# Scan output returned by scatters through the inverse rank, and earlier loads of the next input

## The chip, the cores and the metric

The kernel runs on one core of one Trainium2 chip. The core has TensorE (PE; its weight loads are shown apart as PEld), VectorE (DVE), ScalarE (ACT), GpSimd (POOL) and SyncE (SP), and 16 DMA engines that all of them share. The engines run their own instruction streams and wait for each other through semaphores. The metric is the device time of one execution in microseconds (us), as the median of three runs.

## The reference

The input is x, 8 images of 512 channels on a 32 x 32 grid (1024 tokens), float32. Four layers follow each other, each added to its input: `x = x + layer(gn(x))`, where `gn` normalises over 32 groups of channels.

- L0: a 5 x 5 map of correlations of each token with its neighbours is put beside the 512 channels, and a 1 x 1 convolution with ReLU follows.
- L1, the layer of this change: a projection to 3 x 512 channels (an input of the scan, a residual and a gate, each through SiLU); a convolution over three tokens; then, for each of two heads of 256 channels, the tokens are put in an order that the head's Moebius parameters give (`perm`), a selective scan with 8 states runs over them, and the result is put back in token order:

```
x_h = _gather_last(x_h, perm[None, :, None, :])
...
y_h = _selective_scan(x_h, dt, A, B_t, C_t, Dparam)
inv = jnp.argsort(perm, axis=-1)
y_h = _gather_last(y_h, inv[None, :, None, :])
y = y * jax.nn.silu(gate) + res
```

  Then an output projection with SiLU.
- L2 and L3: 1 x 1 convolutions with a bias.

The order depends on the parameters alone, so it is the same for all 8 images.

## The kernel before

Images are worked one after the other: image 0, then a loop of three passes over two images each (images 1 to 6), then image 7. Channels lie in `KC` = 4 chunks of 128 partitions, tokens in `NT` = 8 tiles of 128; `P` = 128, `DH` = 256 channels a head, `HEADS` = 2. x of the current image is in `X[z]`; the other buffer `X[1 - z]` is scratch for the scan's factors (`pfac`, `qfac`, `pT`, `qT`, one chunk each) until the next image's x is loaded into it. Large products are made in three passes of half-width parts (`passes`, L1522); the scan's products are in float32. Everything that TensorE does runs through one helper line, L1500, but for transposes. TensorE fills its waits in the scan with pieces of the input projection (`piece`, `filler`).

**Into scan order.** Once a token's row is complete (256 channels and 17 scan parameters, `ROW` numbers), GpSimd scatters the rows of each head to DRAM, eight indirect DMAs of 128 rows a head (L450); the destination of a row is `rank[token]`. SP loads each head back in scan order with one DMA (L353, 1092 KB) into `rows4[:, h]`.

**The scan.** `scan_sums`, `factor_rows`, `scan_inner` and `scan_y` on TensorE, with `scan_states` on DVE (the last of it is L1457, which adds `diag`, made by GpSimd in `diagonal(h)`, L456). `scan_y(h)` gives four pairs of tiles; ACT evicts each pair to `yscan`, a view of `buf_b` (L696, semaphore `y_ev`).

**Back to token order.** SP stores each pair of tiles to `d_y[h]`, in scan order (L357, semaphore `y_out`), four stores a head. When all four have landed, GpSimd gathers the rows by `rank`, eight indirect DMAs a head (L467), into `ytok[h]`, a view of the same SBUF as `rows4[:, h]`. Semaphores `y_in{h}{half}` count them by halves of four tiles. TensorE's `y_chunk(k, half)` (L1788) waits for `y_in{k // 2}{half}` and transposes four tiles back to channels: k = 0, 1 are head 0, k = 2, 3 are head 1. DVE multiplies the result with the gate (L1246) and adds the residual (L1248); the output projection reads that. `y_chunk(0, 0)` comes right behind `scan_y(1)`; `y_chunk(2, 0)` comes behind some of the input and output projection, and `y_chunk(2, 1)` later still.

**x of the next image.** SP loads its four chunks (512 KB each) behind the last `scan_y` product (`y_mm` 8), L363. In images 1 to 6 the next image's statistics come from an earlier load of their own (`early`), so only the normalisation on ACT (L556, L559) reads these chunks. Image 0 has no early load, and DVE takes the next image's statistics from them (`input_stats`, L882).

GpSimd's queue, in the order of its code: scatters of both heads, `diagonal(0)`, `diagonal(1)`, `gather(0)`, `gather(1)`, then memsets and small powers. SP's: rows of both heads, eight stores, four loads of x, the correlation's traffic of the next image, and stores of the output. In image 0 GpSimd waits for `p_rank` before each head's scatters, since the rank is still being counted on DVE.

Of the kernel before, what the change touches and what calls it, by code (L numbers as in the profile page):

```python
# [32 lines left out]
def constants():  # L33

    v = np.arange(P)
    parts = {}
    parts["ident"] = np.eye(P)
    parts["upto"] = v[:, None] <= v[None, :]
    parts["after"] = v[:, None] > v[None, :]
    same8 = (v[:, None] // T8) == (v[None, :] // T8)  # L40
    parts["same8"] = same8
    parts["after8"] = same8 & (v[:, None] > v[None, :])
    parts["group_mean"] = ((v[:, None] // 16) == (v[None, :] // 16)) / 16.0
    parts["ones"] = np.ones((P, P))
    blocks = [(s, size) for size in (128, 64, 32, 16) for s in range(0, P, size)]
    left, right = np.zeros((P, HEADS, G)), np.zeros((P, HEADS, G))
    keep = np.ones((P, HEADS))
    for h in range(HEADS):
        groups = [g for g in range(G) if g != FAR_GROUP[h]]
        for g, (s, size) in zip(groups, blocks):  # L50
            left[s:s + size // 2, h, g] = 1
            right[s + size // 2:s + size, h, g] = 1
        left[:, h, FAR_GROUP[h]] = right[:, h, FAR_GROUP[h]] = 1
        keep[FAR_GROUP[h] * S:(FAR_GROUP[h] + 1) * S, h] = 0
    parts["left"], parts["right"] = left, right
    parts["off_left"], parts["off_right"] = BIG * (1 - left), BIG * (1 - right)
    parts["keep"] = keep
    parts["within8"] = (v[:, None] % T8) <= np.arange(T8)[None, :]
    parts["eq8"] = (v[:, None] % T8) == np.arange(T8)[None, :]
    parts["block16"] = (v[:, None] // T8) == np.arange(P // T8)[None, :]  # L60
    n = np.arange(N).reshape(NT, P).T
    y, x = n // W, n % W
    inside = np.zeros((P, NT, 5, 5))
    for r in range(5):
        for c in range(5):
            inside[:, :, r, c] = ((y + r - 2 >= 0) & (y + r - 2 < H) & (x + c - 2 >= 0) & (x + c - 2 < W))
    parts["inside"] = inside

    step = np.arange(W - 1, dtype=np.float32) / np.float32(W - 1)
    line = np.concatenate([np.float32(-1) * (np.float32(1) - step) + step, [np.float32(1)]]).astype(np.float32)  # L70
    parts["grid"] = np.concatenate([line[x], line[y]], axis=1)
    at, cols = {}, []
    pos = 0
    for name, a in parts.items():
        a = np.asarray(a, np.float32).reshape(P, -1)
        at[name] = (pos, a.shape[1])
        pos += a.shape[1]
        cols.append(a)
    return at, np.concatenate(cols, axis=1)


def build(nc, d):
    at, packed = constants()
    with ExitStack() as ctx:
# [43 lines left out]
        rank = sb("rank", [P, HEADS, NT], I32)  # L128
        deq8 = sb("deq8", [P, HEADS, T8])
# [30 lines left out]
        def scratch(z):  # L160
# [31 lines left out]
        d_scan = [nc.dram_tensor(f"d_scan{h}", (N, ROW), F32, kind="Internal").ap() for h in range(HEADS)]  # L192
        d_score = [nc.dram_tensor(f"d_score{h}", (P, NT), F32, kind="Internal").ap() for h in range(HEADS)]
# [13 lines left out]
            yt_mm y_gate y_res silu2 half_in""".split()  # L207
# [12 lines left out]
                   y_out0=64, y_out1=64, y_in00=8 * NT, y_in01=8 * NT, y_in10=8 * NT, y_in11=8 * NT, yt_mm=2 * KC, y_gate=2 * KC, y_res=2 * KC, silu2=8)  # L220
# [67 lines left out]
        def _(eng):  # L288
# [49 lines left out]
            def image(m, z, last=False):  # L338
# [15 lines left out]
                for h in range(HEADS):  # L354
                    for j in range(4):
                        wait(eng, "y_ev", m, 4 * h + j + 1)
                        eng.dma_start(d_y[h].rearrange("(c p) r -> p c r", p=P)[:, 2 * j:2 * j + 2, :],  # L357
                                      yscan[:, h, 2 * j:2 * j + 2, :]).then_inc(s[f"y_out{h}"], 16)
                if not last:

                    wait(eng, "y_mm", m, 4 * HEADS)
                    for k in range(KC):
                        eng.dma_start(X[1 - z][:, k, :], d["x"][bass.ds(m + 1, 1), k * P:(k + 1) * P, :].rearrange("a p n -> (a p) n")).then_inc(s["x_in"], 16)  # L363
# [21 lines left out]
        def _(eng):  # L385
# [40 lines left out]

            def image(m, z, last=False):
# [15 lines left out]
                for h in range(HEADS):  # L443
# [5 lines left out]
                    for t in range(NT):  # L449
                        eng.indirect_dma_start(d_scan[h], bass.IndirectOffsetOnAxis(ap=rank[:, h, t:t + 1], axis=0),  # L450
                                               rows4[:, h, t, :], None).then_inc(s[f"scattered{h}"], 16)
                def diagonal(h):
# [8 lines left out]
                def gather(h):  # L461

                    wait(eng, f"y_out{h}", m, 64)
                    wait(eng, "y_mm", m, 4 * (h + 1))
                    eng.nop(nofuse=True)
                    for t in range(NT):
                        eng.indirect_dma_start(ytok[h][:, t, :], None, d_y[h],  # L467
                                               bass.IndirectOffsetOnAxis(ap=rank[:, h, t:t + 1], axis=0)).then_inc(s[f"y_in{h}{2 * t // NT}"], 16)

                diagonal(0)  # L470
                diagonal(1)
                gather(0)
                gather(1)
# [39 lines left out]
        def _(eng):  # L513
# [33 lines left out]
            def normalize(m, g, k, x, by_chunk=False):  # L547
# [5 lines left out]
                if k == 0 and g == 2:  # L553
                    wait(eng, "y_out0", m, 64)
                    wait(eng, "y_out1", m, 64)
# [942 lines left out]
        def _(eng):  # L1498
# [114 lines left out]
            def image(m, z, last=False):  # L1613
# [163 lines left out]
                def y_chunk(k, half):  # L1777
# [5 lines left out]
                    wait(eng, f"y_in{k // 2}{half}", m, 8 * NT)  # L1783
# [175 lines left out]
```

## Time and profile before

| | |
|---|---|
| median of 3 runs | 1817.06 us (1812.06 to 1821.29) |
| the profiled execution | 1825.13 us |
| its span in the profile | 1823.3 us |
| TensorE busy | 1719.2 us, 94% |
| VectorE, ScalarE, GpSimd busy | 1088.6, 866.5, 416.0 us |
| memory | 140.15 MB moved, mean 77 GB/s |

Times in the profile count from the span's start. Image 0's scan lies at about 150 to 230 us, and the later ones follow at intervals of some 217 us: image 2 has its scan output at 619 to 660 us, image 3 at 835 to 877 us. A row of a timeline gives start, duration, engine, line, operation, what it writes and reads, and in brackets the idle time of the engine before it with what ended it. Ends of matmuls are modelled, so a busy TensorE is not one at its peak, and its own idle time is what can be won.

### The profile page before, as it was taken

Reading aid. Unit: us, or ns where it says so; the run is one execution under the profiler, and the core shown is the slowest. Engines: PE = TensorE matmul, PEld = TensorE weight load, DVE = VectorE, ACT = ScalarE, POOL = GpSimd, SP = SyncE. Lnnn points to the kernel's source line nnn. Section 1 sums busy time; section 2 is a strip of 40 time slices with the busy share of each in tenths; the row PEclk is TensorE's granted clock in tenths of the full one; section 3 lists DMA queues with packets and bytes.
Section 4 is the critical chain, followed back from the end, with each engine's and each line's share of the span. In section 5 each row is a group of like instructions: output and inputs, shape, how many; then the busy total and the mean of one; then the engine's idle time right before and its main releaser. Section 6 shows DMA issues by size and latency. Waiting matters only on the chain.

```text
span 1823.3 us, 23722 instructions
## 1 busy us (share of the span) xinstructions
PE 1719.2 (94%) x8573; PEld 949.8 (52%) x8573; DVE 1088.6 (60%) x2136; ACT 866.5 (48%) x1057; POOL 416.0 (23%) x425
## 2 busy tenths in 40 slices
PE   4498999999999999999999999999999999999998
PEld 3154554555545554556545565455554555555643
DVE  6778575555754666546665547555575466652665
ACT  4665245554255534454534643555425653445432
POOL 0403301133022321132120430113302232113220
PEclk9799999999999999999999999999999999999999
DMA  6203410233112231133201341023311132112201
GB/s 210 80 1 99 139 39 16 87 113 116 38 68 68 97 103 34 71 110 108 69 14 70 122 139 39 13 89 115 116 38 65 65 101 102 39 46 93 76 24 46
DMA packets 124055, 140.15 MB, mean 77 GB/s; under 512 B 52243, under 2 KB 101459, under 8 KB 123934
## 3 DMA queue, kind: packets, MB, share of 16 engines
q1 hardware_dynamic: 109886, 103.18, 17.8%
q0 software_dynamic: 12288, 34.68, 5.7%
q8 instruction: 72, 1.18, 0.3%
q10 hardware_dynamic: 1760, 0.71, 0.2%
q14 instruction: 49, 0.40, 0.1%
HBM read 78.52 MB, written 60.01 MB: 76 GB/s over the span
## 4 chain that ended last, share of the span: by engine, by line
PE 67%; DVE 10%; issue 9%; DMA 5%; ACT 4%; POOL 2%; another core or an unknown queue 2%; SPq 0%; DVEq 0%; POOLq 0%; ACTq 0%
PE bank L1500 64%; DMA rows<-d_scan 2%; DMA rows<-d_norm 1%; DVE bn L882 1%; POOL d_scan L450 1%; PE bank L1721 1%; DVE gate L1246 1%; PE bank L1788 1%; DVE gate L1060 1%; PE bank L1666 1%; DMA d_scan<-rows,rank 1%; DVE res L1180 1%; DVE res L1178 1%; DVE x_even L1152 1%
## 5 line engine op out<-in xcount | busy, mean ns | idle before, releaser
L1500 PE MATMUL bank<-buf_a,win_hi 128*128 128x512 f16 x1536 | 461.6, 382 | 8.1 <-DVE buf_a L954 8.1
L1500 PE MATMUL bank<-buf_a,win_lo 128*128 128x512 f16 x768 | 293.2, 382 | 0.0
L1500 PE MATMUL bank<-buf_b,w_hi 128*128 128x512 f16 x960 | 287.5, 381 | 2.8 <-DVE buf_b L954 2.8
L1500 PEld LDWEIGHTS bank<-buf_a,win_hi 128*128 128x128 f16 x1536 | 150.2, 99 | 190.0 <-issue 22.0
L1500 PE MATMUL bank<-gate,w_out 128*128 128x512 f32 x512 | 229.2, 594 | 5.1 <-DVE gate L1248 5.1
L450 POOL DMA_INDIRECT d_scan<-rows,rank x128 | 125.9, 984 | 357.4 <-DVE rows L1215 314.6
L1500 PE MATMUL bank<-buf_b,w_lo 128*128 128x512 f16 x480 | 183.3, 382 | 0.0
L1500 PE MATMUL bank<-buf_a,w_hi 128*128 128x512 f16 x576 | 171.3, 379 | 1.4 <-DVE x_odd L1152 1.4
L1500 PEld LDWEIGHTS bank<-gate,w_out 128*128 128x128 f32 x512 | 94.4, 190 | 112.3 <-issue 98.8
L1500 PEld LDWEIGHTS bank<-buf_b,w_hi 128*128 128x128 f16 x960 | 93.9, 99 | 112.4 <-DVE buf_b L954 3.5
L467 POOL DMA_INDIRECT rows<-d_y,rank x128 | 121.8, 952 | 133.1 <-DMA d_y<-buf_b 97.6
L1500 PEld LDWEIGHTS bank<-buf_a,win_lo 128*128 128x128 f16 x768 | 75.7, 99 | 92.4 <-issue 3.0
L1246 DVE TENSOR_TENSOR gate<-bank,gate 128x512 f32<-128x512 f32 x64 | 43.9, 685 | 130.0 <-PE bank L1788 90.2
L605 ACT ACTIVATE res<-bank,par 128x512 f32<-128x512 f32 x64 | 48.6, 775 | 139.4 <-issue 77.0
L394 POOL TENSOR_TENSOR st<-st,minus_half 128x4 f32<-128x4 f32 x30 | 30.9, 1029 | 343.1 <-DVE st L940 257.0
L1500 PE MATMUL bank<-buf_a,w_lo 128*128 128x512 f16 x288 | 109.1, 379 | 0.0
L954 DVE TENSOR_TENSOR buf_a<-work,buf_a 128x1024 f16<-128x1024 f32 x68 | 83.0, 1221 | 28.9 <-ACT work L559 28.6
L954 DVE TENSOR_TENSOR buf_b<-work,buf_b 128x1024 f16<-128x1024 f32 x60 | 73.3, 1222 | 41.9 <-ACT work L559 33.4
L605 ACT ACTIVATE buf_b<-bank,par 128x512 f32<-128x512 f32 x64 | 49.7, 776 | 91.1 <-PE bank L1500 91.1
L1500 PEld LDWEIGHTS bank<-buf_a,w_hi 128*128 128x128 f16 x576 | 56.0, 99 | 64.3 <-DVE x_odd L1152 1.8
L594 ACT ACTIVATE work<-bank,par 128x512 f32<-128x512 f32 x64 | 43.2, 683 | 93.1 <-PE bank L1500 93.1
L578 ACT ACTIVATE corr<-bank 96x512 f16<-96x512 f32 x16 | 9.5, 591 | 158.1 <-PE bank L1568 158.1
(227 smaller groups left out, 2921.2 us busy)
## 6 DMA issues: line engine op xcount, KB each, us to landing
rows<-d_scan SPq DMA_DIRECT2D x16, 1092.0 KB, 5.9
d_y<-buf_b SPq DMA_DIRECT2D x64, 256.0 KB, 2.1
work<-in_x SPq DMA_DIRECT2D x24, 512.0 KB, 4.6
d_gram<-rows SPq DMA_DIRECT2D x32, 260.0 KB, 2.4
x_even<-in_x SPq DMA_DIRECT2D x16, 512.0 KB
x_odd<-in_x SPq DMA_DIRECT2D x16, 512.0 KB
out_x<-x_even SPq DMA_DIRECT2D x16, 512.0 KB, 2.7
out_x<-x_odd SPq DMA_DIRECT2D x16, 512.0 KB, 2.6
```

Source lines behind the costliest of these rows:

```text
L394: eng.tensor_tensor(st[g][:, :, 4], st[g][:, :, 3], minus_half.broadcast_to([P, KC]), ALU.pow).then_inc(s[f"gn_rstd{g}"], 1)
L450: eng.indirect_dma_start(d_scan[h], bass.IndirectOffsetOnAxis(ap=rank[:, h, t:t + 1], axis=0), rows4[:, h, t, :], None).then_inc(s[f"scatt ...
L467: eng.indirect_dma_start(ytok[h][:, t, :], None, d_y[h], bass.IndirectOffsetOnAxis(ap=rank[:, h, t:t + 1], axis=0)).then_inc(s[f"y_in{h}{2 ...
L594: act(tmp[:, u % 3, :], ps[out_bank[u]][:, :], ACT.Silu, bias=par[:, BOUT + o:BOUT + o + 1]).then_inc(s["out_evac"], 1)
L605: act(dst, ps[in_bank[q]][:, :], ACT.Silu, bias=par[:, col:col + 1], scale=inv("in")).then_inc(s["in_evac"], 1)
L882: eng.bn_stats(bn[g][:, k, half, :], x[:, k, half * HALF:(half + 1) * HALF]).then_inc(s[f"gn_raw{g}"], 1)
L954: TT(lo[:, k, :], normed[:, k % 2, :], hi[:, k, :], ALU.subtract).then_inc(s[f"gn_split{g}"], 1)
L1060: TS(cmp_row[:, :, start:start + n], others, own[:, t:t + 1], 0.0, op, ALU.add, counts[:, a, q:q + 1]).then_inc(s["p_count"], 1)
L1152: STT(X[z][:, o, c], ps[(l2_bank if stage == 2 else l3_bank)[u]][:, :], par[:, INV + stage:INV + stage + 1], X[z][:, o, c], ALU.mult, ALU. ...
L1178: STT(dst, src[:, 0:N], w[0], dst, ALU.mult, ALU.add).then_inc(s["conv_mac"], 1)
L1246: TT(gate[:, k, c], ps[yt_bank[k][half]][:, :], gate[:, k, c], ALU.mult).then_inc(s["y_gate"], 1)
L1500: return eng.matmul(out, lhsT, rhs, start=start, stop=stop, skip_group_check=True, **kw)
```

## The change

GpSimd no longer gathers. `y_scatter(h, j)` waits for one eviction and scatters its two tiles of 128 rows from `yscan` to `d_y[h]`, at the token's own place. The index is `order`, the inverse of `rank`, in scan order: entry p of tile c is the token at that place of the scan. SP then loads a head of `d_y` in token order with two plain DMAs of 512 KB, one for each `y_in` semaphore (`y_load(h)`), when all eight scatters of the head have landed. The eight stores on SP go. On GpSimd the first two pairs of head 0 are placed in front of `diagonal(1)`.

SP loads chunks 0 to 2 of the next x after `y_load(0)` and `dh_mm` 8 (the last product that reads `pfac`; `qfac` and `pT` are done by then too), chunk 3 after `y_mm` 8, and `y_load(1)` after that.

In image 0 alone `order` is made: GpSimd scatters the token numbers (a new constant, `token`, rows of 8 bytes) by `rank` to `d_order`, 16 indirect DMAs in three places, and SP loads both heads from there.

```diff
+    parts["token"] = np.repeat(n[:, :, None], 2, axis=2).astype(np.int32).view(np.float32)
...
+        order = sb("order", [P, HEADS, NT, 2], I32)
...
-                for h in range(HEADS):
-                    for j in range(4):
-                        wait(eng, "y_ev", m, 4 * h + j + 1)
-                        eng.dma_start(d_y[h].rearrange("(c p) r -> p c r", p=P)[:, 2 * j:2 * j + 2, :],
-                                      yscan[:, h, 2 * j:2 * j + 2, :]).then_inc(s[f"y_out{h}"], 16)
+                if first:
+                    eng.wait_ge(s["order_out"], 16 * NT * HEADS)
+                    for h in range(HEADS):
+                        eng.dma_start(order[:, h], d_order[h].rearrange("(c p) r -> p c r", p=P)).then_inc(s["order_in"], 16)
+
+                def y_load(h):
+
+                    wait(eng, f"y_out{h}", m, 16 * NT)
+                    for half in range(2):
+                        t = slice(half * NT // 2, (half + 1) * NT // 2)
+                        eng.dma_start(ytok[h][:, t, :], d_y[h].rearrange("(t p) r -> p t r", p=P)[:, t, :]).then_inc(s[f"y_in{h}{half}"], 16)
+
+                def x_load(k):
+
+                    eng.dma_start(X[1 - z][:, k, :], d["x"][bass.ds(m + 1, 1), k * P:(k + 1) * P, :].rearrange("a p n -> (a p) n")).then_inc(s["x_in"], 16)
+
+                y_load(0)
                 if not last:
-
+                    wait(eng, "dh_mm", m, 4 * HEADS)
+                    for k in range(KC - 1):
+                        x_load(k)
                     wait(eng, "y_mm", m, 4 * HEADS)
-                    for k in range(KC):
-                        eng.dma_start(X[1 - z][:, k, :], d["x"][bass.ds(m + 1, 1), k * P:(k + 1) * P, :].rearrange("a p n -> (a p) n")).then_inc(s["x_in"], 16)
+                    x_load(KC - 1)
+                y_load(1)
+                if not last:
                     correlation(m + 1)
...
+            def order_out(h, tiles):
+
+                for t in tiles:
+                    eng.indirect_dma_start(d_order[h], bass.IndirectOffsetOnAxis(ap=rank[:, h, t:t + 1], axis=0),
+                                           const("token")[:, 2 * t:2 * t + 2].bitcast(I32), None).then_inc(s["order_out"], 16)
...
+                    if first:
+                        order_out(0, range(5 * h, 5 + 3 * h))
...
-                def gather(h):
-
-                    wait(eng, f"y_out{h}", m, 64)
-                    wait(eng, "y_mm", m, 4 * (h + 1))
+                def y_scatter(h, j):
+
+                    wait(eng, "y_ev", m, 4 * h + j + 1)
                     eng.nop(nofuse=True)
-                    for t in range(NT):
-                        eng.indirect_dma_start(ytok[h][:, t, :], None, d_y[h],
-                                               bass.IndirectOffsetOnAxis(ap=rank[:, h, t:t + 1], axis=0)).then_inc(s[f"y_in{h}{2 * t // NT}"], 16)
+                    for c in (2 * j, 2 * j + 1):
+                        eng.indirect_dma_start(d_y[h], bass.IndirectOffsetOnAxis(ap=order[:, h, c, 0:1], axis=0),
+                                               yscan[:, h, c, :], None).then_inc(s[f"y_out{h}"], 16)
 
                 diagonal(0)
+                if first:
+                    order_out(1, range(NT))
+                    eng.wait_ge(s["order_in"], 16 * HEADS)
+                y_scatter(0, 0)
+                y_scatter(0, 1)
                 diagonal(1)
-                gather(0)
-                gather(1)
+                y_scatter(0, 2)
+                y_scatter(0, 3)
+                for j in range(4):
+                    y_scatter(1, j)
```

The counts of the semaphores follow: `y_out` is now 16 a scatter, and ACT's wait for it before the third normalisation and TensorE's wait for `y_in` are adapted to that.

## Rows read from the trace of the kernel before

**Rows 1.** The page's part 1: busy us (share of the span) and instructions.
```profile
PE 1719.2 (94%) x8573; PEld 949.8 (52%) x8573; DVE 1088.6 (60%) x2136; ACT 866.5 (48%) x1057; POOL 416.0 (23%) x425
```

**Rows 2.** Stretches: us, busy of each engine, granted clock, DMA share, GB/s.
```profile
220.00:230.00 10.00, 8.34 (x27) 4.03 (x26) 8.05 (x21) 1.45 (x3) 2.05 (x7) 1.00 0.09 25
625.00:842.00 217.00, 212.42 (x1071) 117.78 (x1070) 126.87 (x242) 104.53 (x128) 50.16 (x52) 1.00 0.25 78
```

**Rows 3.** Waits of TensorE, 625 to 680 us: total us, times, longest.
```profile
PE bank L1500 <- DVE gate L1248: 0.5, 1, 0.5
PE bank L1500 <- issue: 0.5, 1, 0.5
```

**Rows 4.** Waits of all engines over the whole span.
```profile
POOL rows L467 <- DMA d_y<-buf_b: 97.6, 16, 10.4
...
PEld bank L1788 <- issue: 12.7, 48, 0.3
```

**Rows 5.** Timeline of ScalarE: evictions of the scan output in images 2 and 3.
```profile
619.08 0.60 ACT L696 ACTIVATE buf_b<-bank 128x512 f32<-128x512 f32 x1
...
639.41 0.60 ACT L696 ACTIVATE buf_b<-bank 128x512 f32<-128x512 f32 x1 [1.92 <-PE bank L1500]
...
854.88 0.60 ACT L696 ACTIVATE buf_b<-bank 128x512 f32<-128x512 f32 x1 [0.52 <-issue]
```

**Rows 6.** Timeline of weight loads: the transposes of L1788 in images 2 and 3.
```profile
643.47 1.92 PEld L1788 LDWEIGHTS bank<-cst,rows 128*128 128x128 f32 x16
...
655.30 0.14 PEld L1788 LDWEIGHTS bank<-cst,rows 128*128 128x128 f32 x1 [0.24 <-issue]
...
660.47 0.14 PEld L1788 LDWEIGHTS bank<-cst,rows 128*128 128x128 f32 x1 [0.24 <-issue]
...
871.48 0.14 PEld L1788 LDWEIGHTS bank<-cst,rows 128*128 128x128 f32 x1 [0.24 <-issue]
```

**Rows 7.** Timeline of image 2: scatters into scan order, before and behind them.
```profile
575.80 0.36 DVE L1215 TENSOR_TENSOR rows<-rows 128x64 f32<-128x64 f32 x2
...
577.00 1.06 POOL L450 DMA_INDIRECT d_scan<-rows,rank  x1 [37.13 <-DVE rows L1215]
...
597.79 0.96 POOL L450 DMA_INDIRECT d_scan<-rows,rank  x1 [0.30 <-issue]
...
600.29 0.38 SPq L353 DMA_DIRECT2D rows<-d_scan  x1
```

**Rows 8.** Timeline of image 2: `diagonal(1)`, its reader, and two gathers of head 1.
```profile
623.68 1.97 POOL L456 TENSOR_TENSOR work<-md,cst 128x1024 f32<-128x1024 f32 x1 [13.52 <-DVE md L1432]
...
634.00 1.27 DVE L1457 TENSOR_TENSOR work<-bank,work 128x512 f32<-128x512 f32 x2
...
648.89 0.94 POOL L467 DMA_INDIRECT rows<-d_y,rank  x1 [0.30 <-issue]
...
651.38 0.95 POOL L467 DMA_INDIRECT rows<-d_y,rank  x1 [0.30 <-issue]
```

**Rows 9.** DMA issues at 570.8, 571.3, 600.3 and 702.9 us: KB, us to landing.
```profile
work<-in_x SPq DMA_DIRECT2D x1, 512.0 KB, 3.3
work<-in_x SPq DMA_DIRECT2D x1, 512.0 KB, 4.1
rows<-d_scan SPq DMA_DIRECT2D x1, 1092.0 KB, 5.8
rows<-d_norm SPq DMA_DIRECT2D x1, 532.0 KB, 3.8
```

**Rows 10.** Timeline of image 0: GpSimd, the first transpose, and DVE behind x.
```profile
152.29 0.96 POOL L450 DMA_INDIRECT d_scan<-rows,rank  x1 [7.13 <-DVE rank L1069]
...
166.91 1.96 POOL L456 TENSOR_TENSOR work<-md,cst 128x1024 f32<-128x1024 f32 x1 [3.62 <-DVE md L1432]
...
206.62 1.92 PEld L1788 LDWEIGHTS bank<-cst,rows 128*128 128x128 f32 x16
...
216.37 2.47 DVE L882 BATCH_NORM_STATS2 bn<-x_odd 128x6 f32<-128x512 f32 x4 [3.50 <-DMA x_odd<-in_x]
```

More of the change, by code:

```diff
@@ L192, in build @@
         d_scan = [nc.dram_tensor(f"d_scan{h}", (N, ROW), F32, kind="Internal").ap() for h in range(HEADS)]
+        d_order = [nc.dram_tensor(f"d_order{h}", (N, 2), I32, kind="Internal").ap() for h in range(HEADS)]
         d_score = [nc.dram_tensor(f"d_score{h}", (P, NT), F32, kind="Internal").ap() for h in range(HEADS)]
@@ L206, in build @@
             fac_mv fac_mm fac_arg fac_exp fac_gam fac_pq fac_8 fac_diag fac_tp fac_ptq mm_m m_ev dh_mm h_zero h_st y_mm y_ev y_out0 y_out1 y_in00 y_in01 y_in10 y_in11
-            yt_mm y_gate y_res silu2 half_in""".split()
+            yt_mm y_gate y_res silu2 half_in order_out order_in""".split()
         gn_names = [f"gn_{what}{g}" for g in range(4) for what in ("raw", "stat", "sum", "var", "rstd", "bias", "hi", "norm", "split")]
@@ L219, in build @@
                    m_ev=2 * HEADS, dh_mm=4 * HEADS, h_zero=1, h_st=7 * HEADS, y_mm=4 * HEADS, y_ev=4 * HEADS,
-                   y_out0=64, y_out1=64, y_in00=8 * NT, y_in01=8 * NT, y_in10=8 * NT, y_in11=8 * NT, yt_mm=2 * KC, y_gate=2 * KC, y_res=2 * KC, silu2=8)
+                   y_out0=16 * NT, y_out1=16 * NT, y_in00=16, y_in01=16, y_in10=16, y_in11=16, yt_mm=2 * KC, y_gate=2 * KC, y_res=2 * KC, silu2=8)
         for g in range(4):
@@ L553, in normalize @@
                 if k == 0 and g == 2:
-                    wait(eng, "y_out0", m, 64)
-                    wait(eng, "y_out1", m, 64)
+                    wait(eng, "y_out0", m, 16 * NT)
+                    wait(eng, "y_out1", m, 16 * NT)
                 act((a_hi if g == 3 and by_chunk else gn_hi_of[g])[:, k, :], x[:, k, :], ACT.Identity, bias=st[g][:, k, 5:6], scale=st[g][:, k, 4:5]).then_inc(s[f"gn_hi{g}"], 1)
@@ L1782, in y_chunk @@
                         wait(eng, "y_ev", m, 4 * HEADS)
-                    wait(eng, f"y_in{k // 2}{half}", m, 8 * NT)
+                    wait(eng, f"y_in{k // 2}{half}", m, 16)
                     if k >= 2:
```

## The prediction

> **What bounds the kernel now.** First the page's busy times [rows 1]: TensorE is busy for 1719.2 of 1823.3 us. Its clock is not the issue: in a steady image the granted clock is 1.00, the 2.4 GHz level [rows 2]. A window of 217 us over one whole image (the third, called image 2) has TensorE busy for 212.4 us [rows 2]. Some 4.6 us an image are idle, and this is the most that a steady image can win.
>
> Next the waits of TensorE in image 2 while the scan output travels [rows 3]: 0.5 us for a gate multiplication, 0.5 us for issue, none for the returning rows. Over the whole run the transposes of L1788 waited 12.7 us in 48 places, each time "issue" and at most 0.3 us [rows 4]. GpSimd waited 97.6 us for the d_y stores [rows 4], which looks like the cost to remove, but TensorE names GpSimd's rows nowhere. The return path is hidden today. The question is whether it stays hidden, because the change also alters its length.
>
> **Head 0.** The first eviction of head 0 ends at 619.68 [rows 5]; SP stores, GpSimd gathers, and TensorE reaches `y_chunk(0, 0)` at 643.47 [rows 6]. After the change each pair of scatters follows its eviction. The trace has scatters of the same kind: L450 moves 128 rows an instruction, 0.96 us and 0.30 us between two, so eight last 7 x 1.26 + 0.96 = 9.8 us; the first starts 0.84 us after the last work that it waits for (576.16 to 577.00); and SP reacts 1.54 us after the end of the last one (598.75 to 600.29) [rows 7]. The rows now have 1024 instead of 1092 bytes, so I take these durations as they are. Head 0: start 619.68 + 0.84 = 620.5, four scatters to 625.3, `diagonal(1)` (1.97 us [rows 8]) to 627.6, four more to 632.7, plus 1.54 = 634.2, when SP issues two loads. `diagonal(1)` moves from 623.68 to about 625.6; its reader L1457 starts at 634.00 [rows 8], so 8.4 us of cover shrink to 6.4. Cost 0; without that cover, 2 us.
>
> For the plain load of half a head (512 KB) I have: 532 KB in rows of 532 bytes, 3.8 us from issue to landing; 512 KB in 4 KB rows 3.3 us, and the next one, issued 0.5 us later, 4.1 us; a whole head (1092 KB) 5.8 us [rows 9]. I take 3.8 us for the first half, since its 1 KB rows are nearest to the first kind, and 5.6 for both. Head 0 is in by 640, 3 us before TensorE wants it. Cost 0.
>
> **Head 1, the tight one.** From the end of its first eviction to `y_chunk(2, 0)` there are 15.3 us in image 2 (640.01 to 655.30) and 16.0 in image 3 (855.48 to 871.48) [rows 5, 6]. The same two places read in the other images give 15.2 for images 0, 1, 5 and 7 and 16.4 for 4 and 6. Today the fourth gather is issued by 652.33 [rows 8] and its half is in before TensorE comes. After the change half 0 needs all eight scatters and then a load: 0.84 + 9.8 + 0.3 (three more waits, one in front of a pair, 0.1 us each as my guess below the 0.30 us pause) + 1.54 + 3.8 + 0.05 for the last semaphore = 16.3 us. TensorE stands 1.1 us in images 0, 1, 2, 5 and 7, 0.3 in image 3, and 0 in images 4 and 6: 5.8 us. TensorE works in order and is full behind this point, so a steady image doesn't take a stall back. Half 1 is wanted 5.2 us later (660.47 [rows 6]) and lands 1.8 us after half 0: no cost. What is late next are the gates of chunks 2 and 3 and the out projection behind them, by the same time.
>
> Bounds: with the load at 3.3 us and no pause between pairs, 15.5 us, a stall of 0.3 in five images, 1.5 us in all. With the load at 5.8 us, 18.3 us: 3.1 x 5 + 2.3 + 1.9 x 2 = 21.6 us.
>
> The page "DMA: Bandwidth & Descriptors" of the Trainium skill (Anatomy of one DMA) gives about 2.0 us plus the bytes at 436 GB/s, an estimate of 3.2 us for this load. This case's loads are slower than that rule [rows 9]; by the rule the stall would be 0.5 in five images, 2.5 us in all.
>
> **The x loads.** Three of four chunks leave after `dh_mm` 8 instead of `y_mm` 8, on SP right behind `y_load(0)`, so at about 635 instead of 644; the fourth stays; all are in before `y_load(1)` is issued near 652. In a steady image TensorE waits for nothing that comes from x there [rows 3]: gain 0. SP loses eight stores and gains four loads an image, with no work queued behind them that is near: cost 0. Without the early start the 2 MB would lie before `y_load(1)` all the same, so it isn't a cover that the sum needs.
>
> **Image 0.** Sixteen extra scatters of 8-byte rows. The first five fit into the 7.13 us in which GpSimd waits for the rank of head 1 (5 x 1.26 = 6.3) [rows 10]: cost 0. Three more, 3.8 us, lie in the 3.62 us before `diagonal(0)` [rows 10]: 0.2 us, covered. Eight more run from 169.4 to 179.2; then 1.54 us, then SP's two loads of 1024 tiny rows each. The trace has none; the nearest take 3.8 us (the 532-byte rows, as many) and 3.3 at the least [rows 9]. I take 3.8 plus 0.4 for the second, so `order` is in at 184.9. Head 0's scatters start near 185.8, end at 198.2 with the diagonal inside them; half 0 lands at 203.6 and half 1 at 205.4, against TensorE's 206.62 [rows 10]. Cost 0.2 as a middle, 0 to 2. The other way, DVE waited until 216.37 for x [rows 10], its statistics delayed the gates, and TensorE lost 1.7 us (8.34 of 10 busy from 220 to 230 [rows 2]). x now lands some 3 us sooner, which pays for this image's own 1.1 us. The constants' load grows by 8 KB once: nothing.
>
> **Sum.** 5.8 - 1.1 + 0.2 = +4.9, say +5 us on the profiled execution's 1825.13 us (span 1823.3), which lies 0.4% above the median of 1817.06. Taken over as a difference: 1822 us. A change of 0.5%, about 9 us, is what a measurement of this kernel can tell from none. So my forecast is "no change that can be told, on the slow side".
>
> **Rivals.**
> A, the forecast: stalls of about 1 us, total -1 to +12 us, 1816 to 1829. Chance 0.48, of which 0.13 falls beyond +9, since that needs only 16.8 us of path instead of 16.3.
> B, slower: both halves of a head land together, after 5.8 us. Then the 21.6 us above less 1.5 in image 0: +20, 1837 us. It decides once the first half takes over 4.3 us. For it: the whole-head load of 5.8 us. Against it: of two loads issued 0.5 us apart the first landed 1.3 us before the second [rows 9]. The same page of the Trainium skill (Queues, rings and completion order) says that each DMA engine consumes one queue's descriptors in ring order, which agrees. Chance 0.20.
> C: no stall, because half 0 comes in 3.3 us or less, and image 0 gains its 1.7 us: 1815 to 1818. Chance 0.18.
> D, faster: TensorE's idle time shrinks, since next image's normalisation no longer meets a late x and DVE's gates come sooner. It needs 1.1 of the 4.6 idle us in every image; no wait in [rows 3] names a load. 1806 us; chance 0.07.
> E, slower: DVE holds GpSimd off. Head 1's scatters run from 640.9 to 651, over the four gate additions of L1248, which read two SBUF tiles. Held 0.69 us by each, +2.8 us an image on top of A: 1844. Against it: the gather at 648.89 took 0.94 us over such an addition, and the one at 651.38, without one, 0.95 [rows 8]. The Trainium skill's "SBUF — State Buffer" describes an exclusive port lock between the two; this trace does not show it on indirect DMAs. Chance 0.07.
>
> **Numbers.** Same: 0.35 + 0.18 = 0.53. Slower: 0.13 + 0.20 + 0.07 = 0.40. Faster: 0.07. The likeliest case's own range is 1816 to 1829. The range for 8 in 10 takes in C below and most of B above: 1813 to 1839.
>
> **What the profile after would show.** Right: no wait before `y_chunk(0, 0)`; a wait of 0 to 1.5 us before `y_chunk(2, 0)` in most images, released by a DMA; scatters of 0.95 us with 0.3 to 0.4 us between; head 1's last one ending 10.7 to 11.1 us after its first eviction; half 0 landing 3.3 to 4.1 us after issue. Wrong: pairs that stand over 0.6 us apart, a half landing after 5 us (B), scatters over 1.2 us beside the gates (E), or idle TensorE time gone that now reads "gate" or "issue" (D). What would make me most wrong is a scatter whose write to HBM lands late because 2.5 MB of loads are queued beside it: all of head 0's loads and x are then in flight while head 1 is scattered.

## Result, and the profile after

| | before | after |
|---|---|---|
| median of 20 runs each | 1816.03 us (1812.06 to 1821.29) | 1820.44 us (1817.51 to 1824.05) |
| the profiled execution, its span | 1825.13, 1823.3 us | 1821.2, 1819.4 us |

The ratio is 1.0027, with a 95% interval from 1.0018 to 1.0035: 4.9 us slower (0.0027 x 1816). The forecast was +5 us, "no change that can be told, on the slow side". The sum came out, but the steps did not: its three terms were off by 2, 3 and 5 us, and the errors cancelled.

The shown execution of before was a long one for its kernel (1825.13 where the timed ones took 1812 to 1821). A kernel that has the change's constant, tensors and semaphores but uses none of them (`e4_alloc_only` below, 1816.5 us) is therefore the better picture of before, and its trace is used beside it. Lines moved: L474 scatters into scan order (L450 before), L448 makes `order`, L492 is `y_scatter`, L367 `y_load`, L371 `x_load`, L1820 the transposes of `y_chunk` (L1788), L1422 the scan's masks, on which TensorE waits when a scan begins.

The page of the kernel after, parts 1 and 6: GpSimd has sixteen instructions more than in [rows 1], and a load of half a head takes 4.4 us as a median over both halves.

```profile
PE 1717.9 (94%) x8573; PEld 951.3 (52%) x8573; DVE 1090.1 (60%) x2136; ACT 867.6 (48%) x1057; POOL 437.9 (24%) x441
...
rows<-d_y SPq DMA_DIRECT2D x32, 512.0 KB, 4.4
```

Waits of the kernel after over the whole span (us in total, times, longest):

```profile
POOL d_y L492 <- ACT buf_b L728: 125.0, 23, 10.6
...
PE bank L1532 <- DVE scan_tmp L1422: 16.3, 8, 3.7
...
PEld bank L1820 <- DMA rows<-d_y: 3.8, 8, 0.9
```

The second of these three waits, the one for the masks, in the trace of `e4_alloc_only`, that is, before:

```profile
PE bank L1503 <- DVE scan_tmp L1393: 9.3, 8, 2.1
```

GpSimd's 97.6 us of waiting for stores [rows 4] are gone and replaced by 125.0 us of waiting for evictions, and neither matters. The new wait for returning rows is 3.8 us: 0.8 to 0.9 in images 0, 2 and 7, and in the other five 0.24, which is the usual time between two issues. The larger difference stands at the start of the scans: 16.3 instead of 9.3 us, which the prediction had at nothing. (The trace of before itself names the masks for two of these waits only, 2.1 us; the same eight gaps of TensorE sum to 7.9 us there.)

**Head 1 in image 2.** Timeline of the kernel after, the stretch of [rows 5, 6, 8]:

```profile
633.91 0.60 ACT L728 ACTIVATE buf_b<-bank 128x512 f32<-128x512 f32 x1 [0.52 <-PE bank L1532]
...
635.26 0.96 POOL L492 DMA_INDIRECT d_y<-buf_b,order  x1 [6.73 <-ACT buf_b L728]
636.53 0.96 POOL L492 DMA_INDIRECT d_y<-buf_b,order  x1 [0.31 <-ACT buf_b L728]
...
644.12 0.96 POOL L492 DMA_INDIRECT d_y<-buf_b,order  x1 [0.30 <-issue]
...
638.68 1.92 PEld L1820 LDWEIGHTS bank<-cst,rows 128*128 128x128 f32 x16
...
647.45 0.94 SPq L367 DMA_DIRECT2D rows<-d_y  x2
...
651.21 0.86 PEld L1820 LDWEIGHTS bank<-cst,rows 128*128 128x128 f32 x8 [0.92 <-DMA rows<-d_y]
...
656.00 0.14 PEld L1820 LDWEIGHTS bank<-cst,rows 128*128 128x128 f32 x1 [0.24 <-issue]
```

The path from the end of the first eviction (634.51) is read off step by step: 0.75 us to the first scatter, 9.82 for eight of them (the waits between pairs add nothing), 2.37 until SP issues, then the landings of the two halves, from the view of DMA issues:

```profile
rows<-d_y SPq DMA_DIRECT2D x1, 512.0 KB, 3.7
rows<-d_y SPq DMA_DIRECT2D x1, 512.0 KB, 4.7
```

That is 16.7 us to the weight load at 651.21. `y_chunk(0, 0)` at 638.68 did not wait, and `y_chunk(2, 0)` would have come 11.8 us behind it, as it does in images without a stall, at 650.5.

Image 2 is not the usual one. The same reading in all eight images, in us (path and TensorE are counted from the end of the first eviction of head 1, TensorE up to `y_chunk(2, 0)`):

| image | first scatter to end of the eighth | SP issues after | path to the landing | TensorE, unstalled | stall |
|---|---|---|---|---|---|
| 1, 3, 4, 5, 6 | 9.8 | 1.5 | 15.7 to 15.9 | 16.0 | 0 |
| 2 | 9.8 | 2.4 | 16.7 | 16.0 | 0.7 |
| 0, 7 | 10.5 | 1.5 | 16.5 | 15.9 | 0.6 each |

In images 0 and 7 the scatters themselves took 0.7 us longer. The fifth one started while DVE was adding two SBUF tiles for the gate, and took 1.46 us instead of 0.96; the next three, each started in the end of such an addition, took 1.02. Kernel after, image 7:

```profile
1726.52 0.69 DVE L1280 TENSOR_TENSOR gate<-gate,res 128x512 f32<-128x512 f32 x1
...
1726.59 1.46 POOL L492 DMA_INDIRECT d_y<-buf_b,order  x1 [0.30 <-issue]
```

It ended 0.84 us after the addition's end. In image 2 each addition began after the scatter beside it (640.34 against 640.33), and all eight took 0.96. Why SP came 0.9 us later in image 2 is open; `e1_after_again` has 1.5 us there.

### The profile page after: what moved, and what is told of

It is laid out like the page before. It is cut to its first block, busy times and chain, and to the rows that moved or that the text cites. A ratio compares the mean times of both kernels' runs of the same rounds, so it can differ in the third digit from the quotient of the medians.

```text
span 1819.4 us, 23753 instructions
## 1 busy us (share of the span) xinstructions
PE 1717.9 (94%) x8573; PEld 951.3 (52%) x8573; DVE 1090.1 (60%) x2136; ACT 867.6 (48%) x1057; POOL 437.9 (24%) x441
## 4 chain that ended last, share of the span: by engine, by line
PE 68%; DVE 10%; DMA 7%; issue 6%; POOL 4%; ACT 4%; DVEq 0%; SPq 0%; POOLq 0%; ACTq 0%
PE bank L1532 65%; DMA rows<-d_scan 3%; POOL d_scan L474 3%; DMA rows<-d_norm 2%; DVE bn L914 1%; PE bank L1753 1%; DMA d_scan<-rows,rank 1%; PE bank L1820 1%; DVE gate L1278 1%; PE bank L1698 1%; DVE res L1212 1%; DVE res L1210 1%; DVE x_odd L1184 1%; DMA x_even<-in_x 1%; POOL win_lo L530 1%
## 5 line engine op out<-in xcount | busy, mean ns | idle before, releaser
L474 POOL DMA_INDIRECT d_scan<-rows,rank x128 | 125.9, 984 | 354.8 <-DVE rows L1247 315.5
L492 POOL DMA_INDIRECT d_y<-buf_b,order x128 | 128.0, 1000 | 161.2 <-ACT buf_b L728 125.0
```

What stands on the lines that cost most here:

```text
L492: eng.indirect_dma_start(d_y[h], bass.IndirectOffsetOnAxis(ap=order[:, h, c, 0:1], axis=0), yscan[:, h, c, :], None).then_inc(s[f"y_out{h} ...
```

## The experiments

Every kernel was run beside the kernel before on one chip, in three groups and a last one: e1 to e4 (before 1816.25 us), g1 to g4 (1815.32), h2 to h4 (1816.89), i1 (1816.70). Each difference below is the ratio less one, times 1816.

| label | median, us | ratio (95%) | difference, us |
|---|---|---|---|
| e1_after_again | 1820.93 | 1.0027 (1.0018 to 1.0037) | +4.9 |
| e2_x_late | 1839.39 | 1.0133 (1.0112 to 1.0153) | +24.2 |
| e3_gather_x_early | 1811.78 | 0.9978 (0.9967 to 0.9990) | -4.0 |
| e4_alloc_only | 1816.51 | 1.0000 (0.9990 to 1.0010) | 0.0 |
| g1_no_order | 1815.66 | 1.0000 (0.9991 to 1.0010) | 0.0 |
| g2_head1_gather | 1823.44 | 1.0048 (1.0033 to 1.0063) | +8.7 |
| g3_nops | 1820.55 | 1.0030 (1.0020 to 1.0041) | +5.4 |
| g4_order_behind | 1827.05 | 1.0064 (1.0051 to 1.0077) | +11.6 |
| h2_order_unused | 1820.46 | 1.0021 (1.0010 to 1.0032) | +3.8 |
| h3_order_late_unused | 1814.29 | 0.9986 (0.9973 to 0.9998) | -2.5 |
| h4_one_load | 1831.15 | 1.0073 (1.0053 to 1.0093) | +13.3 |
| i1_count_only | 1813.74 | 0.9991 (0.9982 to 1.0000) | -1.6 |

**e1_after_again**: the kernel after, unchanged.

> The changed kernel once more, beside its three parts, so that all are timed against the kernel before on one chip. Ratio 1.003 again, +3 to +7 us. The profile of the change shows only 3.8 us of waits for the rows in front of the transposes and a shorter span than the profile before (1819.4 against 1823.3 us), while the medians say +4.4 us. Theory P (the profile before was a long execution, and the change costs time at places that both profiles hide in their spread) expects this run's span and time near 1820 us again.

It gave the same ratio, and its trace repeats 16.3 us of waits for the masks. Its time and span are near 1820 us again, as expected.

**e3_gather_x_early**: the kernel before with only the earlier x loads, placed before head 1's stores.

```diff
+                    if h and not last:
+                        wait(eng, "dh_mm", m, 4 * HEADS)
+                        for k in range(KC - 1):
+                            x_load(k)
```

> The kernel before with only the early x loads: three chunks behind dh_mm 8, in front of head 1's stores. Theory W expects no change within 2 us, or up to 2 us faster through image 0. Theory X expects about +5 us.

This part alone wins 4.0 us, more than the 2 us expected, and beats both kernels. The gain is made in image 0: in the profiled executions `y_chunk(2, 1)` starts 4.4 us sooner there than in `e4_alloc_only`, and the end of the span is 3.6 us sooner. DVE waits there for x, and this is the row in `e4_alloc_only`:

```profile
214.90 2.47 DVE L885 BATCH_NORM_STATS2 bn<-x_odd 128x6 f32<-128x512 f32 x4 [4.39 <-DMA x_odd<-in_x]
```

and in the kernel after, against 3.50 us until 216.37 in [rows 10]:

```profile
213.59 2.47 DVE L914 BATCH_NORM_STATS2 bn<-x_odd 128x6 f32<-128x512 f32 x4 [0.46 <-DMA x_odd<-in_x]
```

Windows of 5 us behind it, in `e4_alloc_only` (the column behind the five engines is the granted clock):

```profile
215.00:220.00 5.00, 4.18 (x16) 1.97 (x14) 4.99 (x11) 0.00 (x0) 2.51 (x3) 1.00 0.38 106
220.00:225.00 5.00, 3.27 (x6) 1.63 (x7) 3.57 (x10) 0.00 (x0) 1.04 (x1) 0.63 0.02 3
225.00:230.00 5.00, 5.00 (x16) 2.58 (x15) 1.56 (x3) 1.38 (x2) 0.22 (x5) 0.69 0.00 0
```

and in `e3_gather_x_early`:

```profile
220.00:225.00 5.00, 5.00 (x19) 2.73 (x20) 2.73 (x7) 1.38 (x2) 1.41 (x6) 1.00 0.04 13
```

TensorE idled 0.8 us in the first of these windows and 1.7 in the second, and the granted clock shows 0.63 and 0.69 in the second and third, means over a change from the 2.4 to the 1.2 GHz level and back; with x in time TensorE stayed busy at 1.00. From `y_chunk(2, 0)` to `y_chunk(2, 1)` it took 10.6 us in e4, 7.5 in the profiled execution of before, whose clock did not fall, and 5.4 in e3. The prediction read the size off the execution with 7.5.

**e4_alloc_only**: the constant, the tile `order`, the DRAM tensors and the semaphores are added to the kernel before, and nobody uses them.

> The kernel before with only the new constant, the tile order, the DRAM tensors and the two semaphores allocated, none of them used: all addresses behind them move. Theories W and X both expect a ratio of 1.000 within 2 us. Theory L (addresses alone make the difference) expects +4 to +5 us.

Other addresses cost nothing.

**e2_x_late**: the kernel after, all four x loads after `y_mm` 8, still ahead of `y_load(1)`.

```diff
-                    wait(eng, "dh_mm", m, 4 * HEADS)
-                    for k in range(KC - 1):
-                        x_load(k)
                     wait(eng, "y_mm", m, 4 * HEADS)
-                    x_load(KC - 1)
+                    for k in range(KC):
+                        x_load(k)
```

> The changed kernel with all four x chunks loaded behind y_mm 8 again, in front of y_load(1). Theory W (the loss is TensorE's wait before y_chunk(2, 0)) expects no gain: the scatters of head 1 then share the DMA engines with 2 MB of loads, half 0 lands no earlier, 0 to +10 us against the changed kernel. Theory X (the early x loads are what costs, by meeting other transfers or the code of the engines) expects this version back at the kernel before, -4 to -6 us against the changed one.

18.5 us slower than after (1839.39 - 1820.93), where 0 to 10 were expected. The scatters of head 1 now have 2 MB of loads beside them. DMA issues of `e2_x_late` in image 2, 640 to 645 us:

```profile
x_odd<-in_x SPq DMA_DIRECT2D x4, 512.0 KB, 6.0
...
d_y<-buf_b,order POOLq DMA_INDIRECT x5, 6.1
```

Undisturbed scatters of this kind landed 2.4 us after issue. The last one of image 2 took 4.6. SP issues `y_load(1)` at 652.07, 10.1 us behind the start of `y_chunk(0, 0)` at 642.00, where it was 8.8 (638.68 to 647.45), and TensorE waits 20.5 us in all for the rows. This is what the prediction named as most able to make it wrong ("a scatter whose write to HBM lands late because 2.5 MB of loads are queued beside it"). In the kernel after it does not happen: three chunks of x are issued from 631.0, the fourth at 639.1, and all are in before the last scatter of head 1 starts at 644.12. The early x loads, which the prediction called no cover that the sum needs, are one.

**h4_one_load**: the kernel after, head 1 loaded by one DMA of 1 MB on which both halves wait. This is the case of rival B, for head 1.

```diff
+                    if h:
+                        eng.dma_start(ytok[h], d_y[h].rearrange("(t p) r -> p t r", p=P)).then_inc(s["y_in10"], 16)
+                        return
...
-                    wait(eng, f"y_in{k // 2}{half}", m, 16)
+                    wait(eng, f"y_in{k // 2}{0 if k >= 2 else half}", m, 16)
```

> The changed kernel with head 1 loaded by one DMA of 1 MB instead of two of 512 KB, so that y_chunk(2, 0) waits for the whole head. It lengthens the suspected wait alone. From 3.7 us the landing goes to about 5.6; theory W (every us by which the rows come later than TensorE is lost in full, once an image) expects 1.9 us more in each image, +13 to +15 us against the changed kernel, ratio 1.010 to 1.011. If something takes the wait back, less than +5 us.

Its rows, from the views of DMA issues, of waits, and of the timeline:

```profile
rows<-d_y SPq DMA_DIRECT2D x1, 1024.0 KB, 5.5
...
PEld bank L1823 <- DMA rows<-d_y: 16.6, 9, 3.3
...
659.77 0.86 PEld L1823 LDWEIGHTS bank<-cst,rows 128*128 128x128 f32 x8 [1.84 <-DMA rows<-d_y]
```

1.8 us more a load made 8.4 us by ratio over after ((1.0073 - 1.0027) x 1816), near 1.0 an image and not 1.8; 13 to 15 us were expected. Part of it is slack, and part of a stall is given back at once: in most images it takes 13.2 instead of 11.8 us from `y_chunk(0, 0)` to `(2, 0)`, and from there to `(2, 1)` 4.8 instead of 5.2. The prediction said that "a steady image doesn't take a stall back"; it takes back 0.4 us of each.

**g1_no_order**: the kernel after without the making of `order`: the scatters take the constant token numbers as index, so the output is not put back in token order, while amount and shape of every transfer of the scan output stay (its rows go to consecutive places).

```diff
-                        eng.indirect_dma_start(d_y[h], bass.IndirectOffsetOnAxis(ap=order[:, h, c, 0:1], axis=0),
+                        eng.indirect_dma_start(d_y[h], bass.IndirectOffsetOnAxis(ap=const("token")[:, 2 * c:2 * c + 1].bitcast(I32), axis=0),
```

> The changed kernel without the making of order: it takes the constant token in its place (so the scan output goes back without the permutation), and image 0 has no extra scatters and loads. In image 0 the load of head 0's rows took 8.6 to 9.1 us from issue beside the 8-byte scatters, against 5.7 without them. Theory I (image 0's order making costs) expects -2 to -3 us against the changed kernel, that load back at 5.7 us and the first transposes of the scan at 164 instead of 166.6 us. Theory W (TensorE's waits for the returned rows are all) expects no change.

All 4.9 us are gone, where 2 to 3 were expected. Its wait for the masks is back to 8.6 us, while the wait for rows, 3.1 us, is still there:

```profile
PE bank L1522 <- DVE scan_tmp L1412: 8.6, 7, 2.5
...
PEld bank L1810 <- DMA rows<-d_y: 3.1, 8, 0.9
```

So the new way back together with x early equals before, and against e3 the new way back costs 4.0 us (±2.8, since each ratio is known to some 2 us, in different groups).

**g2_head1_gather**: the kernel after, head 1 by four stores and eight gathers as before.

> The changed kernel with head 1 brought back the old way (four stores, eight gathers), head 0 by scatters, x and order as in the change. Theory W expects the waits in front of y_chunk(2, 0) gone and -3 to -5 us. Theory I expects no change. If the pause of 1.76 us in GpSimd's scatters of images 4 and 7 moves as well, another -3 us.

The waits should have gone and 3 to 5 us with them; instead it is 3.8 us slower than after, and the waits grew: 8.2 us at the weight loads, released by the gathers, 4.4 of them in image 0. Waits, and DMA issues in image 0 from 203.9 us:

```profile
PEld bank L1828 <- DMA rows<-d_y,rank: 8.2, 7, 4.4
...
x_odd<-in_x SPq DMA_DIRECT2D x2, 512.0 KB, 7.9
d_y<-buf_b SPq DMA_DIRECT2D x4, 256.0 KB, 7.9
```

The stores stood on SP behind two loads of rows and three chunks of x, and took 7.9 us in image 0 and up to 5.2 in image 2, where e3's took 2.6. It therefore doesn't tell what head 1's scatters cost; it tells that this queue has no room for small urgent stores.

**g3_nops**: the kernel after with 32 empty instructions ahead of the images on GpSimd, to see whether the pause below follows the instruction stream.

> The changed kernel with 32 empty instructions in GpSimd's stream ahead of the images. GpSimd paused 1.76 us between the second and third scatter of head 0 in images 4 and 7, in all three kernels with the new stream, and in none of the three with the old one. Theory G (the pause belongs to a place in the instruction stream, and the longer stream moved it onto the path to the scan) expects the pauses elsewhere, and -2 to -3 us against the changed kernel if they fall into idle time. If the pause has to do with transfers in flight, it stays, and the time too.

Neither the time nor the pause moved. That theory fell.

**g4_order_behind**: the kernel after, all eight scatters of head 0's numbers behind head 1's rows.

```diff
-                        order_out(0, range(5 * h, 5 + 3 * h))
+                        order_out(0, range(8 * h))
```

> The changed kernel with the eight scatters of head 0's token numbers all behind head 1's rows instead of five in front. Theory I, in the form that the small scatters slow the load of head 0's rows because they run beside it, expects that load back at 5.7 us and the start of the scan 3 us sooner, but diagonal(0) and all that follows on GpSimd 6.3 us later: -2 to +2 us in all.

The load of head 0's rows, which has the 8-byte scatters beside it in the kernel after, is quick again. DMA issue of `rows<-d_scan` in image 0, kernel after:

```profile
rows<-d_scan SPq DMA_DIRECT2D x1, 1092.0 KB, 8.5
```

and `g4_order_behind` (the same in e4):

```profile
rows<-d_scan SPq DMA_DIRECT2D x1, 1092.0 KB, 5.7
```

But `diagonal(0)` and `order` come later, the transposes at 208.9 instead of 206.9, and it lost 6.7 us more, where at most 2 were expected. The waits for the masks fell by 3 us in image 0 (0.2 instead of 3.0) and the time did not follow.

**h2_order_unused and h3_order_late_unused**: e3 plus the making of `order`, which nobody reads (the gathers stay). In h2 it stands where the change has it; in h3 the sixteen scatters come late in image 0's queue.

```diff
-                    if first:
-                        order_out(0, range(5 * h, 5 + 3 * h))
...
-                if first:
-                    order_out(1, range(NT))
-                    eng.wait_ge(s["order_in"], 16 * HEADS)
...
+                    if first:
+                        order_out(0, range(NT))
...
+                    if first:
+                        order_out(1, range(NT))
```

> The gathers of the kernel before with the early x loads, and order made in image 0 exactly as in the change, with both waits, but not used. Theory I (making order costs +4.9 us by itself, as leaving it out of the changed kernel gave) expects +4 to +6 us against the gathers with early x, so about the kernel before (ratio 1.000 to 1.001), the load of head 0's rows in image 0 near 9 us instead of 5.7, and GpSimd's long pause at its 146th and 242nd indirect DMA instead of the 114th. If the cost belongs to the scatters of the scan output instead, the ratio stays at 0.998.

> The same as the last, but the sixteen small scatters lie in GpSimd's idle time after image 0's scan (eight behind rstd(m, 2), eight behind norms(m + 1)), and SP loads order at the end of image 0. It splits the cost of making order: the part in image 0's scan is gone, the count of GpSimd's indirect DMAs is the same. If the shifted pause of 1.76 us in images 4 and 7 is the rest, +2 to +3 us against the gathers with early x; if it is all in image 0, 0 us.

On one chip, h2 took 6.2 us more than h3 (1820.46 - 1814.29). So the making itself is cheap, 1.5 us over e3 with an interval that holds zero, and its place is what costs, with the gathers as with the scatters.

h2 also gives the parts a second time, in the other order. Over e3, the early making costs 7.8 us here, where after over g1 gave 4.9; and the new way back costs 1.1 us (after over h2), where g1 over e3 gave 4.0. Each of these is uncertain by some 3 us, so the runs do not say how the 8.9 us divide between the two.

**Where those 5 us lie.** TensorE's waits for the masks in windows over the starts of scans 0, 4 and 7. h2:

```profile
PE bank L1525 <- DVE scan_tmp L1415: 3.8, 1, 3.8
...
PE bank L1525 <- DVE scan_tmp L1415: 1.7, 1, 1.7
...
PE bank L1525 <- DVE scan_tmp L1415: 3.0, 1, 3.0
```

h3:

```profile
PE bank L1524 <- DVE scan_tmp L1414: 0.2, 1, 0.2
...
PE bank L1524 <- DVE scan_tmp L1414: 0.3, 1, 0.3
...
PE bank L1524 <- DVE scan_tmp L1414: 2.2, 1, 2.2
```

It is tempting to add up 3.6 + 1.4 + 0.8 = 5.8 us. The starts of `y_chunk(2, 1)` in the traces tell otherwise for image 0:

| image | e4 (before) | e3 | g1 | after | after - g1 |
|---|---|---|---|---|---|
| 0 | 226.6 | 222.2 | 223.8 | 224.2 | +0.4 |
| 2 | 659.2 | 655.0 | 656.8 | 656.0 | -0.8 |
| 3 | 875.4 | 871.2 | 874.5 | 875.1 | +0.6 |
| 4 | 1089.8 | 1085.6 | 1089.2 | 1091.0 | +1.8 |
| 6 | 1522.4 | 1517.1 | 1520.3 | 1522.5 | +2.2 |
| 7 | 1737.9 | 1734.2 | 1735.7 | 1742.1 | +6.4 |

Image 0 starts its scan 3 us late and ends 0.4 us late: in g1, TensorE waits 2.2 us for DVE a little later (1.2 in e4), and in the kernel after that wait is used up. The last column rises at image 3 (by 1.4), at image 4 (by 1.2) and most at image 7 (by 4.2, of which the wait for the masks is 2.9); with `e1_after_again` in place of after the three steps are 1.4, 2.5 and 2.8. In images 4 and 7 GpSimd pauses between its first two scatters. Kernel after, timeline of GpSimd:

```profile
1008.28 1.04 POOL L474 DMA_INDIRECT d_scan<-rows,rank  x1 [37.11 <-DVE rows L1247]
1011.08 0.96 POOL L474 DMA_INDIRECT d_scan<-rows,rank  x1 [1.76 <-issue]
```

`e4_alloc_only` and h3 have the pause too, among the gathers of images 3 and 4:

```profile
846.13 0.97 POOL L470 DMA_INDIRECT rows<-d_y,rank  x1 [1.64 <-issue]
```

```profile
1058.65 0.96 POOL L487 DMA_INDIRECT rows<-d_y,rank  x1 [1.63 <-issue]
```

The pause is the 146th and the 242nd indirect DMA in after, e1, e2, g2, g3, g4, h2 and h4; the 114th (in g1 also the 210th) in before, e3, e4 and g1; the 162nd in h3. In image 4, all eight kernels of the first kind wait 1.7 to 2.0 us for the masks, and the others 0.3 to 0.5; in image 7 they wait 2.4 to 3.7 and the others 0.8 to 2.2. By the means of the two kinds that is 1.5 us in each of the two images, about 3 us in all, an estimate.

**i1_count_only**: g1 plus sixteen 8-byte scatters in GpSimd's idle time from 81 to 106 us, to bring the pause back without making `order`. The output is again not in token order.

```diff
+                if first:
+                    eng.nop(nofuse=True)
+                    for h in range(HEADS):
+                        for t in range(NT):
+                            eng.indirect_dma_start(d_order[h], bass.IndirectOffsetOnAxis(ap=const("token")[:, 2 * t:2 * t + 1].bitcast(I32), axis=0),
+                                                   const("token")[:, 2 * t:2 * t + 2].bitcast(I32), None).then_inc(s["order_out"], 16)
```

> This is the kernel without the making of order (the one that took 1815.7 us, ratio 1.0000 to before), with sixteen scatters of 8-byte rows put back where nothing of the scan is near: into GpSimd's idle time from 80.6 to 137.9 us of image 0, token numbers to their own place in d_order, which nobody reads (the output is again not put back in token order). Theory P, the place of GpSimd's pause: the 1.7 us pause between two indirect DMAs is the 114th's and the 210th's without the sixteen, in the scatters of the scan output, where it costs nothing, and the 146th's and the 242nd's with them, in the scatters in front of the scans of images 4 and 7. Sixteen more DMAs anywhere early should bring it back there, TensorE's wait for the masks should be some 1.7 us in image 4 (0.4 without) and 2.5 to 3.7 in image 7 (0.8 without) and about 0.2 in image 0, and the time should be 1819 to 1821 us, ratio about 1.0025. Theory M, the making of order inside image 0 (head 0's rows land 3 us late, the scan starts 3 us late): neither is there, so 1815 to 1817 us, ratio 0.9995 to 1.0007, wherever the pause falls. In between, near 1.0012, would say that both have a share, or that the place of the pause is not set by the count alone, which the index of the pause will show.

The pause did not move within the work: it is now the 130th and the 226th, that is, the same scatters of the scan output in images 3 and 6 as in g1. The time stayed too (1.6 us below g1, within the two intervals), against the 1819 to 1821 us of the pause theory, and the wait for the masks is 8.7 us. The number of indirect DMAs thus doesn't set the place, and the run doesn't test what the pause costs at a scan's start. It shows that sixteen such scatters cost nothing where GpSimd is idle.

## Why the forecast was right

1. **Head 0, cost 0: right.** The trace after has no wait before or in `y_chunk(0, 0)`, image 0 included, where it came at 206.88 against 206.62. There it is close: in e1, TensorE stood 0.6 us for head 0's second half.
2. **Head 1, "5.8 us": place right, size wrong.** The path of 16.3 us was near: it took 15.7 to 15.9 us in five images and 16.5 to 16.7 in three. Its steps hold too, "1.54 us" for SP (1.5 in seven images of eight), 3.8 for the landing (3.7 to 3.9), with no pause between pairs where 0.3 was guessed. What was wrong is the other side, "15.2 for images 0, 1, 5 and 7", 15.3 in image 2: it was read off one execution. In `e4_alloc_only`, the same program but for unused tensors, TensorE comes 15.9 or 16.0 us after that eviction in all eight images, and so it does after the change. So five images don't stall, and three do, by 0.6 to 0.7 us: 1.9 us in all, where the forecast had 1.1 in five images. By time, the return path costs 4.0 ± 2.8 (g1 against e3) or 1.1 ± 2.8 (after against h2).
3. **x, "gain 0" in steady images and -1.1 in image 0: place right, size wrong.** It is -4.0 us. The working read its size, 1.7 us, off one execution, in which the clock had not fallen behind the wait, and let only 1.1 of it into the sum.
4. **`order`, "cost 0" for thirteen scatters and 0.2 as a middle: wrong.** It is +4.9 (+7.8 with the gathers). Two steps failed. "The first five fit into the 7.13 us" counts GpSimd's time alone: they lie in the DMA queues beside the load of head 0's rows, which took 8.5 us instead of 5.7, and every later time of the chain was late. Both heads of `order` were in at 187.8 instead of 184.9. Yet that delay was covered, as item 1 and the table say. What costs shows from image 3 on, in images 4 and 7 above all, where the prediction had nothing at all.
5. **The sum** is 4.0 - 4.0 + 4.9 = +4.9, or by h2 1.1 - 4.0 + 7.8, against 5.8 - 1.1 + 0.2. Measured parts along one path must add up to the whole; that the forecast's own three did is chance.

On the rivals: A has the right place of the stalls, at a third of their size. B is excluded, since the first half landed in 3.7 us and the second in 4.7; h4 shows its price as +8.4 over the kernel after, where 15.8 (21.6 - 5.8) had been worked out. C, no stall, holds in five images of eight and fails in three. D is half true: idle time behind a late x did shrink, but in image 0 alone, and e3 shows what it is worth. E is not excluded but true in part: its mechanism is what made the scatters of images 0 and 7 0.7 us longer, a stall of 0.6 in each, where E had 2.8 us in every image. An indirect DMA that starts while DVE adds two SBUF tiles waits for the addition's end; one that starts first does not. The prediction's sentence that the trace of before does not show this was a misreading: the gather at 648.89 had started before the addition beside it (649.11), so it could not tell, and image 3 of the same trace shows the hold:

```profile
863.97 0.69 DVE L1248 TENSOR_TENSOR gate<-gate,res 128x512 f32<-128x512 f32 x1
...
864.33 1.14 POOL L467 DMA_INDIRECT rows<-d_y,rank  x1 [8.48 <-DMA d_y<-buf_b]
```

The Trainium skill's "SBUF — State Buffer" (Who interferes with whom) has a VectorE instruction with two SBUF inputs contend with a GpSimd instruction that reads SBUF, and the second to come wait; these traces agree. The rule of the Trainium skill's "DMA: Bandwidth & Descriptors" (Anatomy of one DMA), which the page states for DMAs that GpSimd issues, gave an estimate of 3.2 us for half a head and gives 4.4 for a whole one; measured were 3.7 and 5.5 for these loads of SP, so the rows were the better source.

What stays open: why the place of the making moves GpSimd's pause by 32 or 48 indirect DMAs, and what makes up all of the +4.9. Kernels with the early making have the pause at a scan's start and take 4.9 (after against g1) or 6.2 us (h2 against h3) more; with late or no making the pause lies among the return transfers. But the longer waits for the masks behind it are only about 3 us, and no run moved the pause alone, so that it is the cause is argued, not shown.

## What to carry to other kernels

Split a change by parts before believing its sum: here the part that wins (x sooner, e3: 0.9978) came with two that together lose twice as much. A tiny transfer is not free because its engine was idle: look at which large load it runs beside, and check whether later stages move too. And both the size of a stall and the slack in front of an engine must be read from more than one execution: here the first was 1.7 us in one and 4 in the median, and the second 15.2 us in one and 16.0 in another.

## What the hardware showed that was not expected

- An indirect DMA of GpSimd that starts while DVE runs an operation with two SBUF inputs is held until that operation is over: most of those held ended 0.8 to 0.9 us behind it, and they took up to 1.46 us instead of 0.96 (after, images 0 and 7; before, image 3, 1.14).
- GpSimd pauses 1.4 to 1.8 us once or twice a run (96 indirect DMAs apart where twice), between the first and the second behind a wait. Neither 32 more instructions (g3) nor sixteen more indirect DMAs ahead (i1) moved it within the work.
- Five scatters of 128 rows of 8 bytes beside a load of 1092 KB made it 8.1 to 9.3 us (after, e1, e2, g2, g3, h2, h4) instead of 5.7 (e3, e4, h3, g4). One such scatter itself landed after 6.7 us, where scatters of 1 KB rows took 2.4.
- 2 MB of loads beside them made scatters of 1 KB rows land after 4.6 to 6.4 us instead of 2.4 (e2, image 2), and stores of 256 KB queued behind loads took 7.9 in image 0 instead of 2.7 (g2 against e3).
